# Order of transposes and pieces, and of their splitting, in the slots of a latent attention kernel

## What is computed

```
x = hidden_states
xn = layernorm(x)
q = xn @ w_q ; k = xn @ w_k ; v = xn @ w_v
lq = xn @ w_lq ; lk = lq @ w_lk ; lv = xn @ w_lv
q, k, lk = rope(q), rope(k), rope(lk)
attn = causal_attention(q, repeat(k, 4), repeat(v, 4))
lat = causal_attention(q, lk, lv)
x = x + attn @ w_o + lat @ w_lo
xn = layernorm(x)
x = x + xn @ W.T + b + lora(xn)
```

## Time and profile before

| What | Value |
|---|---|
| Median of three executions | 2036.75 us (2035.94 to 2037.59) |
| The profiled execution | 2036.75 us |
| Its span, first to last instruction | 2035.0 us |
| TensorE busy, matmuls | 2018.2 us, 99% |
| TensorE busy, weight loads | 1753.1 us, 86% |
| VectorE busy | 1457.1 us, 72% |
| ScalarE busy | 1203.7 us, 59% |
| GpSimd busy | 889.9 us, 44% |
| Share of TensorE in the chain that ended last | 97% |
| Mean granted clock of TensorE | 0.998 |

### The profile page before, as it was taken

One profiled execution on the slowest core, in us unless ns is written; L12 is line 12 of the kernel. 1 busy time (PEld: TensorE's weight loads), 2 busy tenths in 40 slices (PEclk: granted clock), 3 DMA queues, 4 the chain that ended last, 5 costly groups with the idle time before them and its releaser, 6 DMA issues.

```text
span 2035.0 us, 33416 instructions
## 1 busy us (share of the span) xinstructions
PE 2018.2 (99%) x11716; PEld 1753.1 (86%) x11716; DVE 1457.1 (72%) x2884; ACT 1203.7 (59%) x2505; POOL 889.9 (44%) x684
## 2 busy tenths in 40 slices
PE   8999999999999999999999999999999999999989
PEld 7888888888888888888888888888888888888877
DVE  7677776776777767777677776777776776777777
ACT  4666556565565656666566565666566565565651
POOL 5444544444443454444534454444544444443422
PEclk9999999999999999999999999999999999999999
DMA  3111111111111111112111111111111111111031
GB/s 108 47 34 44 48 28 38 34 49 37 38 39 39 33 44 37 44 28 49 33 44 37 39 39 28 49 34 44 48 28 41 32 49 39 37 39 38 23 68 42
DMA packets 101797, 83.78 MB, mean 41 GB/s; under 512 B 28152, under 2 KB 73848, under 8 KB 101632
## 3 DMA queue, kind: packets, MB, share of 16 engines
q1 hardware_dynamic: 101632, 81.65, 15.7%
HBM read 79.26 MB, written 2.36 MB: 40 GB/s over the span
## 4 chain that ended last, share of the span: by engine, by line
PE 97%; DVE 2%; ACT 1%; POOL 0%; issue 0%; DMA 0%; DVEq 0%; ACTq 0%
PE bankT L587 13%; PE scores L514 12%; PE scores L516 12%; PE scores L515 12%; PE bankX L514 9%; PE bankX L516 9%; PE bankX L515 9%; PE bankO L516 7%; PE bankO L515 7%; PE bankO L514 7%; PE scores L707 0%; PE scores L553 0%; DVE rot_half L1124 0%; DVE xnT_lo L1097 0%; ACT probs L876 0%
## 5 line engine op out<-in xcount | busy, mean ns | idle before, releaser
L815 ACT ACTIVATE PT_hi<-bankT 128x512 fp32r<-128x512 f32 (+2 forms) x640 | 337.5, 533 | 310.7 <-PE bankO L516 275.5
L1113 DVE TENSOR_TENSOR PT_lo<-bankT,PT_hi 128x512 fp32r<-128x512 f32 (+2 forms) x640 | 388.1, 607 | 175.7 <-ACT PT_hi L815 173.1
L876 ACT ACTIVATE probs<-probs,nmax 128x128 f32<-128x128 f32 (+7 forms) x512 | 393.9, 771 | 129.8 <-DVE nmax L1107 129.7
L1107 DVE CUSTOM_DVE_ANT_0 probs<-scores,mask 128x128 f32<-128x128 f32 (+7 forms) x512 | 379.2, 750 | 69.3 <-PE scores L516 68.0
L587 PE MATMUL bankT<-ident,probs 128*128 128x128 f32 x2304 | 382.7, 275 | 6.8 <-ACT probs L876 5.0
L587 PEld LDWEIGHTS bankT<-ident,probs 128*128 128x128 f32 x2304 | 279.6, 140 | 67.9 <-DVE PT_lo L1113 11.7
L1369 POOL TENSOR_TENSOR rot<-rot,cos 128x512 f32<-128x512 f32 x144 | 186.9, 1298 | 256.6 <-DVE rot_half L1124 256.6
L1363 POOL TENSOR_TENSOR OT_lo<-o_raw,OT_hi 128x512 fp32r<-128x512 f32 x63 | 98.3, 1560 | 319.9 <-ACT OT_hi L815 319.9
L815 ACT ACTIVATE OT_hi<-o_raw 128x512 fp32r<-128x512 f32 x128 | 146.7, 1146 | 139.7 <-DVE o_raw L1182 139.7
L1371 POOL TENSOR_TENSOR rot<-rot,rot_half 128x512 f32<-128x512 f32 x144 | 199.9, 1388 | 11.3
L1123 DVE TENSOR_TENSOR rot_half<-rot,sin 64x512 f32<-64x512 f32 x144 | 99.5, 691 | 135.3 <-ACT rot L815 132.3
(11 more groups left out here) (304 smaller groups left out, 5334.0 us busy)
## 6 DMA issues: line engine op xcount, KB each, us to landing
inv_b<-inverses SPq DMA_DIRECT2D x128, 256.0 KB, 3.9
stage<-in_L_attn_w_q SPq DMA_DIRECT2D x32, 256.0 KB, 4.8
stage<-in_L_attn_w_lv SPq DMA_DIRECT2D x32, 256.0 KB, 2.9
stage<-in_L_attn_w_o SPq DMA_DIRECT2D x32, 256.0 KB, 3.5
stage<-in_L_attn_w_lo SPq DMA_DIRECT2D x32, 256.0 KB, 2.6
acc<-in_L_attn_hidden_states SPq DMA_DIRECT2D x8, 256.0 KB, 4.9
stage<-in_L_attn_w_k SPq DMA_DIRECT2D x8, 256.0 KB, 5.0
stage<-in_L_attn_w_v SPq DMA_DIRECT2D x8, 256.0 KB, 5.0
```

What stands on the lines that cost most here:

```text
L815: return act.activation(place, src, ACT.Copy)
L876: act.activation(prob_tile(c, t), prob_tile(c, t), ACT.Exp, bias=nmax[:, c, t:t + 1], scale=-1.0, accum_out=rsum[:, c, t:t + 1]).then_inc( ...
L1107: dve.tensor_tensor_reduce(place, src, tile_view(mask[:, S - width:S], c), -SCALE, -MASKED, ALU.add, ALU.min, nmax[:, c, t:t + 1]).then_in ...
L1113: dve.tensor_tensor(pt_place(1, hh, w, j), bankT[j % 2][:, block_columns(c, j):CH], f32(pt_place(0, hh, w, j)), ALU.subtract).then_inc(pt_ ...
```

## The change

In each slot three orders change. On TensorE the transposes of block s + 2 move from behind the piece (and the transposes of the last head's feed-forward weights) to ahead of it. On ScalarE the high part of block s + 2 stands ahead of the exponentials and the piece's copy in every slot that has a block s + 2, not only in those without a piece or with LK or OUT; the copy of LK still stands first. On VectorE the low part of block s + 2 stands ahead of the piece's work in every such slot, not only with Q1; where there is no block s + 2 the piece's work stands where it stood.

```
--- before.py
+++ after.py
@@ -679,13 +679,13 @@
                                 score_tile(no, t % 2, nhh, WINDOWS[nw][0], WINDOWS[nw][1], t)
+                        if s + 2 < BLOCKS[w]:
+                            transpose_block(g, hh, w, s + 2)
                         if s in pieces_of(g, hh, w):
                             piece(g, hh, w, s, *pieces_of(g, hh, w)[s])
                         if w == NW - 1 and not more:
                             for n in JOBS_AT[s]:
                                 ffn_transpose(n)
-                        if s + 2 < BLOCKS[w]:
-                            transpose_block(g, hh, w, s + 2)
@@ -899,7 +899,7 @@
-                        early = s + 2 < BLOCKS[w] and name in ("", "LK", "OUT0", "OUT1")
+                        early = s + 2 < BLOCKS[w]
                         if early:
                             block_hi(g, hh, w, s + 2)
@@ -1206,12 +1206,12 @@
                         here = pieces_of(g, hh, w)
-                        behind = here.get(s, ("", 0)) == ("Q", 1)
+                        behind = s + 2 < BLOCKS[w]
                         if s in here and here[s][0] != "LK" and not behind:
                             piece(g, hh, w, s, *here[s], piece_bank(g, hh, w, s))
                         if s + 2 < BLOCKS[w]:
                             block_lo(g, hh, w, s + 2)
-                        if behind:
+                        if behind and s in here and here[s][0] != "LK":
                             piece(g, hh, w, s, *here[s], piece_bank(g, hh, w, s))
```

## The result

The changed kernel takes 2190.05 us (median of 4 runs, 2188.95 to 2192.18) against 2037.17 us for the kernel before beside it: ratio 1.0752, 95% interval 1.0733 to 1.077. It is slower, by 153 us where 118 were forecast; the time lies inside the stated range. The profiled execution, the slowest of the four, has a span of 2190.4 us, 155.4 more than before.

A forecast was written before the change was run, and what follows sets the result against it. TensorE, busy 2018.2 of 2035.0 us, was taken as the bound. Stalls of 48.4 + 62.9 + 4.0 + 8.4 less 5.8 gave 117.9 us on 2036.75, so 2155 us; range 2127 to 2215.

The forecast's parts named there:

- the step that carried the sum: Slot 0 of windows 1 and 3: waits the piece had hidden become TensorE stalls, 48.4 and 62.9 us.
- earlier transposes give ScalarE nothing: ScalarE's high part waits for products still behind the piece, so its bankO wait (275.5 us) stays; taken as 0.
- One sign that the prediction named as showing it wrong: Whole kernel: TensorE's summed waits and the added time differing by more than 20 us would refute the forecast.
- slot 0 of window 0: Transposes there stall 0.13 us where LK0 used to cover, 31 times: 4.0 us.
- slot 0 of window 1: Transposes of block 2 stall 1.56 us for the low part LV1 used to hide, 31 heads: 48.4 us.
- what LKT_lo gives back: Window 1's stall gives GpSimd time for LKT_lo, returning between 0 and 11.6 us; half taken, 5.8 us.
- slot 0 of window 3: Transposes stall 2.03 us for a low part behind Q0's rotation, formerly hidden by Q1, 31 heads: 62.9 us.
- the old wait of rows 7: Slot 3 of window 3, heads 0 to 2: existing wait for the low part, 0.13 us to be won 24 times.
- slot 2 of window 3, heads 0 to 2: Block 4's transposes wait 0.48 us where OUT0 used to start; net of 0.13 us, 24 times: 8.4 us.
- the step on the clock: Steady-part stalls: no clock fall assumed, after 1.99 us idle near the start without one; 105 us kept as other end.
- The rival that I gave 0.20: Clock falls after window 3's stall, 3.4 us each: 54 us more at half the heads, 2209 us; chance 0.20.
- The banks' rival: VectorE's later add and low half free banks late, mostly hh = 3: 17 to 21 us, 2172 to 2176; chance 0.13.

The follow-up runs named there:

- e6: The kernel before, with the transposes ahead of the piece in slot 0 of window 3 alone: 2118.27 us, ratio 1.0397.
- e7: The kernel before, with the transposes ahead of the piece in slot 0 of window 1 alone: 2090.23 us, ratio 1.0261.
- e5: The changed kernel, but in window 2 VectorE writes the low part of window 3's block 0 before rotating Q0: 2152.43 us, ratio 1.0567.
- e1: The change's TensorE part alone, ScalarE and VectorE ordered as in the kernel before: 2187.81 us, ratio 1.0733.
- e4: The changed kernel with 12 unused transposes of ident in the stalls of slot 0, windows 1 and 3: 2168.02 us, ratio 1.0637.
- e3: The changed kernel, but in slot 0 of every window the transposes stay behind the piece: 2056.22 us, ratio 1.009.
- e10: The changed kernel with ScalarE's splitting of Wk and Wv (hh = 3) moved behind the high parts of window 1's blocks 0 and 1: 2177.4 us, ratio 1.0694.
- e2: The kernel before with only the change's ScalarE and VectorE orders, TensorE's order untouched: 2046.75 us, ratio 1.0044.
- e11: The changed kernel with 5 unused transposes of ident in the stalls of slot 0, windows 1 and 3: 2168.14 us, ratio 1.0643.
- e8: The kernel before with Q1 rotated behind block 3's low part in window 3, and unused turns of ident in the last head's idle: 2032.52 us, ratio 0.9976.

## Why the prediction came out as it did

**Direction and main mechanism** were right, by the step that carried the sum: a wait that lay wholly under a piece is laid bare when the transposes that wait are put ahead of the piece. e6 and e7 show each of the two large terms by itself, e5 that VectorE's low part sets the wait's end. So was the reading that earlier transposes give ScalarE nothing: in e1 its wait for bankO is 271.9 us, as before.

One sign that the prediction named as showing it wrong did come: the sum of TensorE's waits and the added time were to agree within 20 us, and they are 113.2 and 153 us, 40 apart. The clock's 22 us (e4) and the 15 us that the profile counts as busy make up most of that, so the waits themselves were as forecast and the added time was not. The time also lies inside the range only because its upper end allowed for falls of the clock in up to half the heads: without them the range ended at 2176.

**The terms, against what the runs showed**, in us:

| Term | forecast | measured | from |
|---|---|---|---|
| slot 0 of window 0 | 4.0 | 6.9 | windows of the changed kernel |
| slot 0 of window 1, less what LKT_lo gives back | 48.4 - 5.8 = 42.6 | 24 x 1.34 + 7 x 2.05 = 46.5 | e7 |
| slot 0 of window 3, less the old wait of rows 7 | 62.9 - 3.1 = 59.8 | 24 x 1.86 + 7 x 2.01 = 58.7 | e6 |
| slot 2 of window 3, heads 0 to 2 | 24 x 0.48 = 11.5 | 24 x 0.39 = 9.4 | e3 |
| slots 1 and 3 of window 1, heads 0 to 2 | 0 | 24 x 0.24 = 5.8 | e3 |
| windows 2 and 3 of hh = 3 | 0 | 1.1 + 1.5 = 2.6 | e3 |
| 16 falls of the clock | 0 | 11 x 1.61 + 5 x 1.51 = 25.3 | windows with a fall less those without |
| Sum | 117.9 | 155.2 | the span grew by 155.4 |

The measured terms come from several runs, so a part of the close match of the sum is luck. The 25.3 us are those of the profiled execution; by the medians e4 took away 22.

**What failed** is the step on the clock, "I take no fall, since that row is nearest". The row was the idle of 1.99 us near the start; in the steady heads 1.78 us were enough in a third of the cases. And the row was a single case. At the same place the changed kernel idled for 2.42 us and kept its clock, while e10, whose edit does not touch the start, idled as long and lost it. The changed kernel, then e10, each with a row of the table by stretches (columns as in the earlier trace rows, the granted clock 1.00 and 0.57):

```profile
15.45 0.47 PE L514 MATMUL scores<-xnT_hi,Wq_lo 128*128 128x512 f32 x1 [2.42 <-DVE xnT_lo L1097]
15.00:20.00 5.00, 4.55 (x20) 3.79 (x21) 4.49 (x15) 2.86 (x6) 1.29 (x1) 1.00 0.38 99
```

```profile
15.42 0.47 PE L514 MATMUL scores<-xnT_hi,Wq_lo 128*128 128x512 f32 x1 [2.42 <-DVE xnT_lo L1097]
16.00:20.00 4.00, 4.00 (x12) 3.13 (x11) 3.49 (x12) 1.87 (x3) 1.28 (x1) 0.57 0.28 82
```

The rival that I gave 0.20 was true in part: 11 of 31 stalls of window 3 were followed by a fall, and so were 5 in window 1, which it had not named. That these make the 16 falls for which it had given a price is luck. Its price was off as well. A fall was put at 3.4 us after the one of 7 us in the earlier trace rows; here each lasted half as long:

```profile
1410.00:1414.00 4.00, 4.00 (x13) 3.27 (x14) 2.19 (x4) 1.15 (x1) 1.74 (x2) 0.57 0.03 5
```

The stretch lies behind a stall of window 3. Three rows of TensorE from it:

```profile
1410.86 0.63 PE L515 MATMUL bankX<-xnT_lo,Wq_hi 128*128 128x512 f32 x1
1411.29 0.63 PE L516 MATMUL bankX<-xnT_hi,Wq_hi 128*128 128x512 f32 x1
...
1414.02 0.40 PE L514 MATMUL bankX<-xnT_hi,Wq_lo 128*128 128x512 f32 x1
1414.26 0.39 PE L515 MATMUL bankX<-xnT_lo,Wq_hi 128*128 128x512 f32 x1
```

From start to start it is 0.43 us at the 1.2 GHz level and 0.24 at 2.4 GHz, and a window with a fall is 1.5 to 1.6 us longer, not 3.4. The Trainium skill (TensorE: Matmul & The Clock Gate, Part 1), as I had read it, made the low clock a matter of unbroken idleness, so that broken stalls would leave the sum alone. My reading was of its rule alone: under its second failure mode the same part tells of a kernel whose frequent short idle times between groups of matmuls made the clock swing. The measurement decides: stalls of 1.78 us with dense matmuls on both sides brought it down in 40 of 124 cases.

**Two smaller misses.** The sum took one head for all; hh = 3 differs, since ScalarE splits Wk and Wv there, 0.5 us more in 7 heads and most of the 5 falls (e10). And slots 1 and 3 of window 1 were left out (0.24 us, e3). What LKT_lo gives back was sized about right: in e7 the stall is 1.55 us (1.31 us of idle and the 0.24) and the window grows by 1.34, so 0.21 us come back, where 5.8 / 31 = 0.19 were taken. The banks' rival was right in place, and it is 8 us without TensorE's part (e2) and under 3 us with it.

## What to carry to other kernels

When a producer's result must pass through two other engines before TensorE can go on, the work between is the cover, and its place in the order matters more than having the input early. Before moving a waiting instruction ahead of a piece, compare the wait's end with its new start in each kind of slot and each kind of head; one that had shown no idle at all cost 2 us here. On an engine that is otherwise busy without a gap, a short stall can cost nearly double when it brings the clock down (here 1.6 us on top of 2.0), and five useless transposes inside the stall kept it up. And a single stall that left the clock alone is no proof that the next one will: count the cases before pricing such a term at nothing.

## What the runs showed of the hardware

Falls of the clock against the idle time that the profile gives ahead of the transposes, over the steady heads of all profiled executions:

| Idle | where | falls |
|---|---|---|
| 0.78 us | window 3 of e5 | 0 of 31 |
| 1.24 us, behind 5 turns | window 3 of e11 | 0 of 31 |
| 1.31 us | window 1, hh 0 to 2, of e7 | 0 of 24 |
| 1.40 us | window 1, hh 0 to 2, of the changed kernel, e1, e5; all heads of e10 | 0 of 103 |
| 1.57 us, behind 5 turns | window 1, hh = 3, of e11 | 0 of 7 |
| 1.78 us | window 3 of the changed kernel, e1, e6, e10 | 11, 8, 14 and 7, 40 of 124 |
| 2.0 to 2.4 us | window 1, hh = 3, of the changed kernel, e1, e5, e7 | 5, 4, 6 and 5, 20 of 28 |

So with dense matmuls around, idle of up to 1.57 us brought no fall in these runs (0 of 196), and idle of 2.0 us and more mostly did (20 of 28). Which of two equal stalls is hit differs from kernel to kernel, and the count with it, 7 to 14 for the same 31 stalls. It seems to differ between executions of one kernel too, since the four of e10 have mean granted clocks from 0.988 to 0.992. Why was not tried. The low clock lasted 3.41 us each time in the steady heads. In the last head, where work was thin on both sides, it lasted 6.83 us at a time in most kernels, 10.24 us in e2 and 3.41 us in e8; e1 and e10 had a second fall of 3.41 us there.
